# Layer 0's edge stage ends without GpSimd's drain, and the node stage takes its first block in three parts

## The reference

```python
row, col = edge_index                                   # src, dst
tp = fctp_messages(node_features[col], edge_attr, W1, W2, W3, W4)   # one 160-wide message per edge
messages = tp @ Wm + bm
agg = segment_sum(messages, row, num_segments=6250)     # sum the messages of each source node
upd = concatenate([node_features, agg], axis=-1) @ Wu + bu
x = layernorm(x + node_features + upd)                  # then layer 1, of the same general shape
```

## Time and profile before

| What | Value |
|---|---|
| median of three runs | 2670.34 us (2668.51 to 2673.15) |
| time of the profiled execution | 2667.67 us |
| its span in the profile | 2665.9 us |
| TensorE matmul busy | 2427.9 us, 91% |
| VectorE / GpSimd / ScalarE busy | 71% / 59% / 42% |
| mean granted TensorE clock | 0.975 of full speed |

### The profile page before, as it was taken

One profiled execution on the slowest core, in us unless ns is written; L12 is line 12 of the kernel. 1 busy time (PEld: TensorE's weight loads), 2 busy tenths in 40 slices (PEclk: granted clock), 3 DMA queues, 4 the chain that ended last, 5 costly groups with the idle time before them and its releaser, 6 DMA issues. The chain is left out here.

```text
span 2665.9 us, 51473 instructions
## 1 busy us (share of the span) xinstructions
PE 2427.9 (91%) x15408; PEld 2135.8 (80%) x15408; DVE 1887.7 (71%) x5414; ACT 1111.3 (42%) x2570; POOL 1563.5 (59%) x1670
## 2 busy tenths in 40 slices
PE   4999999999999999996899996999999989999997
PEld 2777777777777777776899996888888889888886
DVE  6767766776677667763687776777777777777776
ACT  2666666666666666663122221222222222322222
POOL 0566666666666666666000002777777777777774
PEclk7999999999999999998999998999999999999998
DMA  6799999999888888983788785333333333333332
GB/s 221 263 330 304 313 331 320 319 310 328 293 288 294 292 287 290 294 291 103 280 291 282 275 288 164 102 84 87 85 102 84 88 97 89 87 86 100 86 87 64
DMA packets 416997, 558.63 MB, mean 210 GB/s; under 512 B 73393, under 2 KB 354848, under 8 KB 404133
## 3 DMA queue, kind: packets, MB, share of 16 engines
q10 hardware_dynamic: 217680, 262.22, 29.5%
q0 software_dynamic: 78640, 139.64, 17.7%
q1 hardware_dynamic: 120406, 153.35, 17.6%
HBM read 326.92 MB, written 228.11 MB: 208 GB/s over the span
## 5 line engine op out<-in xcount | busy, mean ns | idle before, releaser
L459 POOL DMA_INDIRECT placed<-message,slots_now x784 | 765.0, 976 | 461.8 <-ACT message L631 275.6
L1494 POOL DMA_INDIRECT f_y<-y_table,b_rec x782 | 758.2, 970 | 252.6 <-issue 178.9
L540 PEld LDWEIGHTS g_bank<-quad_ring,front_work 128*128 128x128 f32 x4704 | 660.6, 190 | 161.7 <-issue 159.2
L540 PE MATMUL g_bank<-quad_ring,front_work 128*128 x4704 | 734.3, 306 | 55.0 <-issue 50.3
L807 DVE SCALAR_TENSOR_TENSOR front_work<-g_bank,quarter_node,front_work 128x512 f32<-128x512 f32 x588 | 404.5, 744 | 136.8 <-issue 59.1
L1688 PE MATMUL e_bank<-f_msg,f_hot 128*126 128x160 f32 x1564 | 349.8, 305 | 36.6 <-DVE f_msg L1573 35.6
L620 ACT COPY front_work<-front_work 32x512 f32<-32x512 f32 x588 | 362.4, 616 | 19.2 <-issue 8.5
L1693 PE MATMUL e_bank<-f_msg,f_hot 128*126 128x160 f32 x1564 | 322.9, 309 | 35.7 <-DVE f_msg L1573 35.0
L1677 PE MATMUL e_bank<-fc,b_hidden 100*128 100x192 f32 x1564 | 321.7, 328 | 0.0
L1570 DVE TENSOR_TENSOR f_msg<-e_bank,f_y 128x256 f32<-128x256 f32 x391 | 165.0, 422 | 217.6 <-issue 186.2
L1774 ACT COPY block_sums<-e_bank 126x320 f32<-126x320 f32 x196 | 83.6, 426 | 551.7 <-PE e_bank L1688 538.5
(11 more groups left out here) (251 smaller groups left out, 3099.2 us busy)
## 6 DMA issues: line engine op xcount, KB each, us to landing
products<-g ACTq DMA_DIRECT2D x49, 2560.0 KB, 9.5
quad_ring<-products ACTq DMA_DIRECT2D x98, 1280.0 KB
big<-placed SPq DMA_DIRECT2D x49, 1458.0 KB, 7.0
b_lengths<-length_parts SPq DMA_DIRECT2D x294, 60.0 KB
placed<-zeros SPq DMA_DIRECT2D x24, 648.0 KB
front_work<-in_e_t SPq DMA_DIRECT2D x196, 64.0 KB
placed<-message,slots_now POOLq DMA_INDIRECT x784, 3.9
f_y<-y_table,b_rec POOLq DMA_INDIRECT x782, 2.5
```

The costliest lines, as they stand in the source:

```text
L459: pool.indirect_dma_start(v.placed[:, :], bass.IndirectOffsetOnAxis(slots_now[tile // SET % SLOT_SETS][:, tile % SET:tile % SET + 1], 0), ...
L540: pe.matmul(bank_now[:, n * D:n * D + D], spread[batch % SPREADS][:, j, q * P:q * P + P], ring[:, bass.ds(slot + j, 1), :].rearrange("p a ...
L1494: pool.indirect_dma_start(f_y[:, at, :], None, v.y_table[:, :], bass.IndirectOffsetOnAxis(b_rec[d % LOAD_RING][:, b % LOADED, 2 * c + n, 0 ...
```

## The change

The edge stage's block is opened with an option that leaves GpSimd's drain instruction out of the barrier at its end; the other four engines' drains and the barrier itself stay, as does SyncE's wait for the last scatters. In the node stage the first block (and it alone) is loaded by three DMAs of six row tiles each, with a semaphore for each; its three selects wait for one part each. For every block, each of the three selects now raises `chosen`, and TensorE waits for it ahead of its row tiles 0, 6 and 12 and no longer once for all 18.

```diff
-        with nc.Block() as block:
+        with nc.Block(no_gpsimd_drain=True) as block:
...
+        opening_in = [v.sem(f"n_opening_in{k}", local) for k in range(2)]
...
-                    if fast:
+                    if fast and b == 0:
+                        sp.wait_ge(agg_full, 1)
+                        rows_of = v.placed[0:SLOTS, :].rearrange("(p j) d -> p j d", p=P)
+                        for g in range(3):
+                            sp.dma_start(placed_rows[0][:, 6 * g:6 * g + 6, :], rows_of[:, 6 * g:6 * g + 6, :]).then_inc(blocks_in[0] if g == 2 else opening_in[g], 16)
+                    elif fast:
...
                 def select(i, k):
                     b = i * N + k
-                    dve.wait_ge(blocks_in[k], i * 16 + 16)
+                    if b:
+                        dve.wait_ge(blocks_in[k], i * 16 + 16)
                     dve.wait_ge(agg_full, b + N - 1)
                     for g in range(3):
+                        if b == 0:
+                            dve.wait_ge(blocks_in[0] if g == 2 else opening_in[g], 16)
                         part = slice(6 * g, 6 * g + 6)
-                        last = dve.tensor_tensor(...)
-                    last.then_inc(chosen, 1)
+                        dve.tensor_tensor(...).then_inc(chosen, 1)
...
                 def sum_rows(i, k):
                     b = i * N + k
-                    pe.wait_ge(chosen, b + 1)
                     pe.wait_ge(sums_turned, b + 1)
                     for j in range(ROWS):
+                        if j % 6 == 0:
+                            pe.wait_ge(chosen, 3 * b + j // 6 + 1)
                         last = pe.matmul(p_agg[k % 2], hot[k % 2][:, j, :], placed_rows[k][:, j, 0:MW], start=(j == 0), stop=(j == ROWS - 1))
```

More of the change, by code:

```diff
@@ L1081, in select @@
                     b = i * N + k
-                    dve.wait_ge(blocks_in[k], i * 16 + 16)
+                    if b:
+                        dve.wait_ge(blocks_in[k], i * 16 + 16)
                     dve.wait_ge(agg_full, b + N - 1)
                     for g in range(3):
+                        if b == 0:
+                            dve.wait_ge(blocks_in[0] if g == 2 else opening_in[g], 16)
                         part = slice(6 * g, 6 * g + 6)
-                        last = dve.tensor_tensor(hot[k % 2][:, part, :], v.count_row[:].unsqueeze(1).broadcast_to([P, 6, P]),
-                                                 placed_rows[k][:, part, RW - 1:RW].broadcast_to([P, 6, P]), ALU.is_equal)
-                    last.then_inc(chosen, 1)
+                        dve.tensor_tensor(hot[k % 2][:, part, :], v.count_row[:].unsqueeze(1).broadcast_to([P, 6, P]),
+                                          placed_rows[k][:, part, RW - 1:RW].broadcast_to([P, 6, P]), ALU.is_equal).then_inc(chosen, 1)
                 def measure(i, k):
```

## The result

| | before | after |
|---|---|---|
| median (us) | 2669.93 (2668.51 to 2673.15, 4 runs) | 2655.21 (2652.48 to 2655.84, 4 runs) |
| profiled execution / span (us) | 2667.67 / 2665.9 | 2655.84 / 2654.1 |

The ratio is 0.9944 [0.9931, 0.9956]: 14.7 us faster, where 10.6 were forecast. Three later comparisons of the same kernel gave 0.9962 [0.9946, 0.9977], 0.9960 [0.9948, 0.9972] and 0.9952 [0.9938, 0.9966], 10.7 to 12.8 us.

A forecast was written before the change was run, and what follows sets the result against it. The prediction took TensorE, nearly full but for a pure wait between edge and node stage, as the bound. Drain 6.3 plus split 4.3 gave 10.6 us, so 2670.34 would become 2659.7 us, range 2655 to 2665.5.

The forecast's parts named there:

- The bound: Between edge and node stage: TensorE is nearly full elsewhere, so only a shorter hole or more node-stage TensorE work changes time.
- The drain: At the edge stage's end: the barrier waits for GpSimd's drain alone; without it the release comes 6.3 us earlier.
- The split: Node stage's first block in thirds: TensorE starts 4.6 us earlier, of which 4.3 us count in the sum.
- The time of one DMA: Block 0's loads by the skill's fit: a third takes 3.1 us, the whole 5.4, making the gain 10.4 us.
- Block 1's rows end the wait: At block 1's start: its rows and one select are ready at 1271.25, after block 0's end at 1271.0.
- Sum at the seam: From edge stage's end into the node stage: 6.3 us from the drain plus 4.3 from the split, 10.6 us.
- Waits by thirds: All node-stage blocks: 98 more TensorE waits cost 0; the bound from the other side was 14.1 us.
- The rival that forecast slower: Node stage: each of the 98 waits costs TensorE one pass, 14.1 us against 10.6 gained, 2673.8 us; chance 0.04.
- The clock rises later: Block 0: TensorE stays at the lower clock throughout, needing 9.8 us; gain 7.8 us, 2662.5 us; chance 0.08.
- I take the whole 10.6: Node stage from block 2 on: row loads keep margins of 1.5 to 3 us, so all 10.6 us are kept.
- later sums at the same distances as now: Node stage's later blocks: their sums follow one another as before, about 6.9 us a block.

The follow-up runs named there:

- e1: The kernel before with only GpSimd's drain left out at the edge stage's end; ratio 0.9971 to the kernel before.
- e10: The changed kernel once more, unaltered, on the same chip as its control; ratio 0.9960 to the kernel before.
- e8: The changed kernel with block 1 too loaded and selected in three parts; one run, no ratio, block 3 at 28.4 us from the last scatter's start.
- e16: The changed kernel once more, unaltered, as a control; ratio 0.9952 to the kernel before.
- e9: The kernel before once more, unaltered, as a control; ratio 0.9999 to the kernel before.
- e3: The kernel before with only the waits changed: each select raises `chosen`, TensorE waits ahead of row tiles 0, 6 and 12; ratio 0.9986 to the kernel before.
- e6: The changed kernel with waits by thirds for block 0 alone, blocks 1 to 48 waiting once; ratio 0.9961 to the kernel before.
- e11: The kernel before with block 0's rows loaded by three DMAs, all waited for together; ratio 1.0000 to the kernel before.
- e12: The kernel before with two more semaphores reserved and never used; ratio 1.0005 to the kernel before.
- e2: The changed kernel with GpSimd's drain put back at the edge stage's end; ratio 0.9975 to the kernel before.
- e13: The kernel before with row loads issued one step earlier from block 8 on; ratio 0.9977 to the kernel before.
- e14: The changed kernel with row loads issued one step earlier from block 8 on; ratio 0.9925 to the kernel before.
- e5: The changed kernel once more, unaltered, for its time and a second profile; ratio 0.9962 to the kernel before.
- e7: The changed kernel with all row loads one step earlier in SyncE's queue (lead 8 for 7); ratio 0.9944 to the kernel before.
- e18: As e17, with the x loads of every later step also ahead of that step's row load; ratio 0.9938 to the kernel before.
- e17: As e14, with block 5's x loads issued before block 8's rows; ratio 0.9927 to the kernel before.
- e4: The kernel before once more, unaltered, for its profile; one run, no ratio, 330.2 us from block 3's start to block 48's end.
- e15: As e14, with block 1's rows too loaded and waited for in three parts; ratio 0.9927 to the kernel before.

## Why the forecast was right, and where it was not

- *The bound* was read rightly: the hole at the seam was a wait, and most of the gain is its shortening.
- *The drain*, 6.3 us: 6.4 at the release in e1. The release came 0.3 us after the last arrival, 0.2 forecast.
- *The split*: TensorE's start moved by 11.5 us in all, 10.9 forecast. The thirds became free 2.1 and 2.3 us apart instead of 1.4, the first of them early; block 0 covered that at the lower clock.
- *The time of one DMA*: the first third landed 3.6 us after its issue; the whole load took 7.1 before. The Trainium skill, "DMA: Bandwidth & Descriptors", section "Anatomy of one DMA", gives 3.1 and 5.4 by its fit, an estimate; both are short, the whole by more. The section states the fit for DMAs that GpSimd issues, which the prediction leaves out, and these are SyncE's. By it the change would gain 10.4, nearer to the 10.1 of the seam than the forecast's 10.6, but by luck: a third came 3.5 us ahead of the whole, where the fit has 2.3 and the forecast 2.8.
- *Block 1's rows end the wait*: shown by the idle 1.25 us and by block 1's start, which stays where it is when block 0 ends 0.9 us later (e10). e8 was meant to test it and did not. By the forecast they were to be the later ones by 0.25 us.
- *Sum at the seam*: 10.6 forecast, 10.1 in the first profile (e10 and e16 against e9: 10.2). Right in size and in its mechanism.
- *Waits by thirds*: cost 0 as far as the runs can tell, by e3 and e6. The rival that forecast slower falls.
- *The clock rises later*: this rival did not come true in the profile after, but block 0 took 7.4 to 8.2 us in twelve of the eighteen profiles of the experiments. In e10 block 3 lost nothing by it: block 1's rows were still the later ones. Without the split the delay is paid: it is why e1 got 5.3 us of its 6.4.
- *What failed* is the step after the sum: "I take the whole 10.6", with "later sums at the same distances as now". It put the node stage behind block 3 at nothing, with no row for it. That stage holds a wait that can change: late row loads, with 31 us of VectorE's idle time and 10.2 of TensorE's in the trace of before, and neither is in the forecast. In the profile after TensorE's wait at `turn_xn` was 6.0 us and the long stretch 4.0 us shorter: 10.1 at the seam and 4.0 behind it stand where the forecast has 10.6 and 0.

Why the long stretch is shorter in the changed kernel is not settled. Excluded are the waits by thirds (e6), the form of block 0's loads (e11) and two semaphores (e12). Neither edit brings it alone: e1 had 332.0 us and e2 327.0. But of the fourteen profiles in which the rows are loaded seven steps ahead, the six with both edits (323.1 to 326.6, e6 and e8 among them) all lie under the eight others (326.9 to 332.0). So some 3 us very probably belong to the two edits together. That they lie in the late rows is likely, since TensorE's busy time did not change and its idle time at `turn_xn` did; e13 and e14 agree with it but don't prove it. The rest of the 14.7 us is the draw of a first comparison with four runs of each kernel, the largest of four comparisons; the later ones gave 10.7 to 12.8 us. Whether the start of TensorE relative to GpSimd's pieces brings the 3 us was not tried.

## What to carry to other kernels

Where a change shortens a hole, look also at what the stage behind it waits for: a wait of up to 1.7 us thirteen times over shows in no slice of the page, but in total it is as large as the gain. Look at when GpSimd's drain ends at a barrier: after its last DMA it took 8.1 us at the one barrier and 8.6 at the other. It costs something only where GpSimd arrives last. At the edge stage's end that was so, and a wait on the last DMAs took its place; at the node stage's end SyncE arrived 2.9 us after the drain was over the earlier trace rows, so there it was free. When a load is moved up in a queue, check what then stands behind it: against the 326.6 us of e5 and e16, rows a step earlier took 11 us off the long stretch in e7 and 13 in e18. In e7 the seam lost 1.7 us of it, since block 0's x loads came late, and in e14 and e17, where later x loads came late, the stretch fell by 6 us only.

## What the runs showed of the hardware

The time from TensorE's start after a long idle to full granted clock was not fixed: 2.8 us (e17) to 6.2 us (e3) in one and the same place of the program, and a start 1.5 us earlier gained nothing by it (e3). In the midst of full work the granted clock fell to half for 3.4 us in four of the twenty profiles (e1, e3, e4, e14), after waits of 1.25 to 2.33 us, while waits of 2.48 and 2.70 us left it at full (e13, e15).

GpSimd's drain ended 8.1 and 8.6 us after its last DMA at the two barriers of the kernel before; without the drain the barrier released 6.4 us earlier (e1).
